# Moving angle and digit work from VectorE to GpSimd, a third pair sum, later low parts and longer values products in a ViT layer kernel

## The reference, cut to what matters

```python
# S4 kernel per token t, for every position l < 1024 and batch c
K = einsum('chn,hnl->chl', Wc, exp(dt_Lambda[..., None] * pos - P_max)).real   # Wc = x * num / den
h = K
h = h + attn(layernorm(h))     # 32 heads of 32, 8 kv groups, rope, causal softmax, T = 128, D = 1024
h = h + ffn(layernorm(h))      # routed low rank: 8 x 16
```

## Time and profile before

| | us |
|---|---|
| median of 3 runs | 2391.71 (2391.33 to 2392.13) |
| the profiled execution, whole | 2390.53 |
| its span | 2388.7 |
| mean granted TensorE clock | 0.988 of full speed |
| busy: TensorE / VectorE / ScalarE / GpSimd | 2276.2 / 1908.7 / 1836.2 / 1708.1 |
| s4_stage, first to last product | 42.2 to about 255.7 |
| layer_stage, first product | 270.0 |
| landing of a 256 KB store of h (DMA list of the page, median) | 3.5 |

### The profile page before, as it was taken

One profiled execution on the slowest core, in us unless ns is written; L12 is line 12 of the kernel. 1 busy time (PEld: TensorE's weight loads), 2 busy tenths in 40 slices (PEclk: granted clock), 3 DMA queues, 4 the chain that ended last, 5 costly groups with the idle time before them and its releaser, 6 DMA issues.

```text
span 2388.7 us, 58825 instructions
## 1 busy us (share of the span) xinstructions
PE 2276.2 (95%) x18704; PEld 1246.2 (52%) x18704; DVE 1908.7 (80%) x7797; ACT 1836.2 (77%) x6269; POOL 1708.1 (72%) x1529
## 2 busy tenths in 40 slices
PE   2999689999999999999999999999999999999986
PEld 2777345555555555555555555555555555555543
DVE  8999578888788788888788878888888878888864
ACT  5998388777877777878777787777787777778773
POOL 1444187877777777777787777777777777777772
PEclk9999899999999999999999999999999999999997
DMA  2888599999999999999999999999999999999984
GB/s 77 263 252 240 135 172 186 187 186 191 189 185 194 188 183 193 191 187 185 191 184 190 192 190 186 189 193 177 192 191 187 187 193 190 180 196 186 184 170 100
DMA packets 1201602, 443.65 MB, mean 186 GB/s; under 512 B 1151622, under 2 KB 1153926, under 8 KB 1201292
## 3 DMA queue, kind: packets, MB, share of 16 engines
q1 hardware_dynamic: 1201284, 439.89, 91.5%
q10 hardware_dynamic: 8, 0.01, 0.0%
HBM read 87.40 MB, written 67.11 MB: 65 GB/s over the span
## 4 chain that ended last, share of the span: by engine, by line
PE 83%; ACT 2%; POOL 1%; DMA 1%; DVE 1%; issue 1%; POOLq 0%; DVEq 0%; ACTq 0%
PE pc L907 13%; PE pb L907 13%; PE pa L907 13%; PE s_ps L920 5%; PE pb L893 4%; PE pb L895 4%; PE pb L894 4%; PE pa L893 4%; PE pa L894 4%; PE pa L895 4%; PE pv_ps L935 4%; PE pd L893 2%; PE pd L895 1%; PE pd L894 1%; DMA pt<-p 1%; ACT pr L1059 1%
## 5 line engine op out<-in xcount | busy, mean ns | idle before, releaser
L1059 ACT ACTIVATE pr<-pr,smin 128x128 f32<-128x128 f32 x2048 | 793.5, 388 | 235.9 <-DVE smin L1205 235.7
L1425 POOL TENSOR_TENSOR pr<-pr,rinv 128x512 f32<-128x512 f32 x512 | 577.0, 1137 | 424.2 <-DVE rinv L1213 413.5
L1205 DVE CUSTOM_DVE_ANT_0 pr<-s_ps,cst 128x128 f32<-128x128 f32 x2048 | 468.7, 286 | 180.2 <-PE s_ps L920 95.7
L1433 POOL TENSOR_TENSOR p<-pr,p 128x512 f16<-128x512 f32 x512 | 590.1, 1158 | 23.9 <-ACT p L1069 13.0
L1069 ACT ACTIVATE p<-pr 128x512 f16<-128x512 f32 x512 | 319.0, 623 | 181.0 <-POOL pr L1425 153.4
L1059 ACT ACTIVATION_READ_ACCUMULATOR pr<-pr,smin 128x1 f32 x2048 | 382.1, 187 | 0.0
L907 PE MATMUL pa<-wkv_hi,xt 128*128 128x512 f16 x1024 | 326.3, 380 | 14.8 <-DMA xt<-xs 14.8
L907 PE MATMUL pb<-wq_hi,xt 128*128 128x512 f16 x1024 | 326.6, 380 | 0.0
L907 PE MATMUL pc<-wq_hi,xt 128*128 128x512 f16 x1024 | 315.0, 379 | 0.0
L642 PE MATMUL hps<-z,xw 128*128 128x256 f32 x848 | 193.7, 388 | 62.1 <-POOL xw L348 42.2
L642 PEld LDWEIGHTS hps<-z,xw 128*128 128x128 f32 x848 | 162.4, 194 | 92.9 <-POOL xw L348 50.5
(11 more groups left out here) (188 smaller groups left out, 4896.2 us busy)
## 6 DMA issues: line engine op xcount, KB each, us to landing
h<-rows SPq DMA_DIRECT2D x128, 256.0 KB, 3.5
h_res<-h SPq DMA_DIRECT2D x64, 512.0 KB, 4.5
out<-rows SPq DMA_DIRECT2D x64, 512.0 KB, 3.2
h_ln<-h SPq DMA_DIRECT2D x63, 512.0 KB, 4.2
pt<-p SPq DMA_TRANSPOSE x512, 3.8
xa<-x SPq DMA_DIRECT2D x16, 256.0 KB, 4.1
xb<-x SPq DMA_DIRECT2D x32, 128.0 KB, 3.8
wst<-wq SPq DMA_DIRECT2D x8, 512.0 KB, 5.7
```

Of the source, the lines that this page charges most:

```text
L1059: last = A.activation(p, p, ACT.Exp, bias=smin[g % 2][:, j:j + 1], scale=-1.0, accum_out=rsum[g % 2][:, j:j + 1])
L1205: V.tensor_tensor_reduce(pr[g % 2][:, cols], s_ps[g % 2][:, cols], mask, 1.0, 3e38, ALU.add, ALU.min, smin[g % 2][:, j:j + 1]).then_inc(ma ...
L1425: nc.gpsimd.tensor_tensor(p3, p3, rinv[g % 2][:, :].unsqueeze(2).broadcast_to([P, HG, P]), ALU.mult).then_inc(p_norm, 1)
L1433: nc.gpsimd.tensor_tensor(p[:, HG * P:], pr[g % 2][:, :], p[:, 0:HG * P], ALU.subtract).then_inc(pl_done, 1)
```

## The change

- Angles are kept in turns instead of radians (zi carries 1/(2 pi)). Bringing them into range is now in_range(): one rounding step (add and subtract MAGIC) and one subtraction; GpSimd does both for chunks 1 to 7, after first_angles. angles() is gone. ScalarE's sines scale by TURN, its square by ROOT_2, so that tables() is one fused step.
- GpSimd makes the second digit product too (digits_m2), right after digits_m1. Its waits on w_lo are gone.
- ON_ACT is 2 in all windows: VectorE makes the xa-products of two tokens a window, ScalarE of two.
- SUM_AT is (0, 1, 2): three of a chunk's eight pairs are summed instead of two.
- pi has two buffers, wst three (WR); low parts are made one window later (LOW_LATER), the last one behind the loop.
- values() in the layer stage waits for its four groups first and then runs 12 matmuls of 512 columns, group g % 4 going to its own 32 partitions of pv_ps; rows of wo are permuted on the host to match.

```diff
-ON_ACT = 3
+WR = 3
+LOW_LATER = 1
+ON_ACT = (2, 2)
...
-        pi = sb("pi", [P, WIN, TOPS, NB])
+        pi = [sb(f"pi{i}", [P, WIN, TOPS, NB]) for i in range(2)]
-        TV, TA, TP = 10, 3, 3
-        SUM_AT = (1, 3)
+        TV, TA, TP = 3, 3, 6
+        SUM_AT = (0, 1, 2)
...
+        def in_range(eng, k):
+            eng.wait_ge(tab_p, TP * k + 1)
+            eng.tensor_scalar(turns[:, :, :], theta[:, :, :], MAGIC, MAGIC, ALU.add, ALU.subtract).then_inc(tab_p, 1)
+            eng.wait_ge(tab_p, TP * k + 2)
+            return eng.tensor_tensor(theta[:, :, :], theta[:, :, :], turns[:, :, :], ALU.subtract)
...
+        def digits_m2(eng, k):
+            return eng.tensor_tensor(dm2[:, :, :].rearrange("p t (s n) -> p t s n", s=2), across(ss, k, 2, DIG),
+                                     tab[k % 2][:, :, :, 0:DIG], ALU.mult)
...
-                    if n >= 2:
-                        sp.wait_ge(w_lo, n - 1)
+                    if n >= WR:
+                        sp.wait_ge(w_lo, n - WR + 1)
...
-                    while loaded < len(PIECES) and PIECES[loaded - 2][0] <= w:
+                    while loaded < len(PIECES) and PIECES[loaded - WR][0] + LOW_LATER <= w + 1:
...
-                        lows = sum(piece[0] < w - 1 for piece in PIECES)
-                        if at in (0, 2, 3) and lows:
-                            pool.wait_ge(w_lo, lows)
                         if at == 0:
-                            pool.wait_ge(tab_v, TV * k + 10)
+                            pool.wait_ge(tab_v, TV * k + 3)
                             first_angles(nc.gpsimd, k + 1).then_inc(tab_p, 1)
+                            in_range(nc.gpsimd, k + 1).then_inc(tab_p, 1)
...
                             digits_m1(nc.gpsimd, k + 1).then_inc(tab_p, 1)
+                            digits_m2(nc.gpsimd, k + 1).then_inc(tab_p, 1)
...
-                    V.tensor_scalar(half[:, :, :], half[:, :, :], -2.0, 1.0, ALU.mult, ALU.add).then_inc(tab_v, 1)
...
-                    V.tensor_tensor(tab[k % 2][:, :, 0, :], expo[:, k * TC:k * TC + TC, :], half[:, :, :],
-                                    ALU.mult).then_inc(tab_v, 1)
+                    V.scalar_tensor_tensor(tab[k % 2][:, :, 0, :], half[:, :, :], 1.0,
+                                           expo[:, k * TC:k * TC + TC, :], ALU.subtract, ALU.mult).then_inc(tab_v, 1)
...
-                    if w >= 1:
-                        dve.wait_ge(xw_done, w)
+                    if w >= 2:
+                        dve.wait_ge(xw_done, w - 1)
...
-                step(V.tensor_scalar(pk, yi, INV_2PI, MAGIC, ALU.mult, ALU.add))
-                step(V.tensor_scalar(pk, pk, MAGIC, None, ALU.subtract))
-                step(V.scalar_tensor_tensor(pf, pk, -TWO_PI_HI, yi, ALU.mult, ALU.add))
-                step(V.scalar_tensor_tensor(pf, pk, -TWO_PI_LO, pf, ALU.mult, ALU.add))
-                step(V.tensor_scalar(pf, pf, PI_SAFE, -PI_SAFE, ALU.min, ALU.max))
+                step(V.tensor_scalar(pk, yi, MAGIC, MAGIC, ALU.add, ALU.subtract))
+                step(V.tensor_tensor(pf, yi, pk, ALU.subtract))
...
-                        if at == 0:
-                            angles(k + 1)
...
-                        if piece[0] == w:
+                        if piece[0] + LOW_LATER == w:
                             weight_lo(n)
+                weight_lo(len(PIECES) - 1)
...
-                        to = slice(P * (g % 4), P * (g % 4) + P)
-                        for n, (v, lo) in enumerate(((v_hi[odd], 0), (v_lo[odd], 0), (v_hi[odd], HG))):
-                            for j in range(HG):
-                                last = pe.matmul(pv_ps[j * HD:(j + 1) * HD, to], v[:, g * HD:(g + 1) * HD],
-                                                 pt[g % RP][:, lo + j, :], start=(n == 0), stop=(n == 2))
+                    for n, (v, lo) in enumerate(((v_hi[odd], 0), (v_lo[odd], 0), (v_hi[odd], HG))):
+                        for g in range(4 * m, 4 * m + 4):
+                            strip = slice(HD * (g % 4), HD * (g % 4) + HD)
+                            last = pe.matmul(pv_ps[strip, :], v[:, g * HD:(g + 1) * HD],
+                                             pt[g % RP][:, lo:lo + HG, :], start=(n == 0), stop=(n == 2))
```

More of the change, by code:

```diff
@@ L150, in s4_stage @@
         cst = W["cst"]
-        re_row, im_row, neg_re_row, row_sign = (cst[:, c:c + 1] for c in (C_RE, C_IM, C_NRE, C_SIGN))
+        re_row, im_row, row_sign = (cst[:, c:c + 1] for c in (C_RE, C_IM, C_SIGN))
         z = [sb(f"z{i}", [P, 4, QROW]) for i in range(ZR)]
@@ L162, in s4_stage @@
         hout = [W[f"rows{i}"] for i in range(HR)]
-        wst = [sb(f"wst{i}", [P, KC * AW]) for i in range(2)]
+        wst = [sb(f"wst{i}", [P, KC * AW]) for i in range(WR)]
         top_r = sb("top_r", [P, TOPS, T])
@@ L212, in s4_stage @@
         x_in = [sem(f"x_in{i}") for i in range(XR)]
-        w_in = [sem(f"w_in{i}") for i in range(2)]
+        w_in = [sem(f"w_in{i}") for i in range(WR)]
         w_hi = sem("w_hi")
@@ L244, in loads_until @@
         def loads_until(n):
-            return 16 * sum(PIECES[i][4] for i in range(n % 2, n + 1, 2))
+            return 16 * sum(PIECES[i][4] for i in range(n % WR, n + 1, WR))
         def weight(name, k):
@@ L289, in load_weight @@
                         piece = src if k is None else src[k * P:k * P + P, :]
-                        sp.dma_start(wst[n % 2][:, at:at + piece.shape[1]], piece).then_inc(w_in[n % 2], 16)
+                        sp.dma_start(wst[n % WR][:, at:at + piece.shape[1]], piece).then_inc(w_in[n % WR], 16)
                         at += piece.shape[1]
@@ L420, in _ @@
                 for w in range(LEAD):
-                    for e in range(ON_ACT):
+                    for e in range(ON_ACT[w % 2]):
                         products(w, e)
@@ L427, in _ @@
                     for e in range(WIN):
-                        if e < ON_ACT and w + LEAD < WINDOWS:
+                        if w + LEAD < WINDOWS and e < ON_ACT[(w + LEAD) % 2]:
                             products(w + LEAD, e)
@@ L449, in step @@
                     dve.wait_ge(pre_v, steps[0])
-                def angles(k):
-                    if k == 0:
-                        first_angles(V, k).then_inc(tab_p, 1)
-                    dve.wait_ge(tab_p, TP * k + 1)
-                    V.tensor_scalar(turns[:, :, :], theta[:, :, :], INV_2PI, MAGIC, ALU.mult, ALU.add).then_inc(tab_v, 1)
-                    dve.wait_ge(tab_v, TV * k + 1)
-                    V.tensor_scalar(turns[:, :, :], turns[:, :, :], MAGIC, None, ALU.subtract).then_inc(tab_v, 1)
-                    dve.wait_ge(tab_v, TV * k + 2)
-                    V.scalar_tensor_tensor(theta[:, :, :], turns[:, :, :], -TWO_PI_HI, theta[:, :, :],
-                                           ALU.mult, ALU.add).then_inc(tab_v, 1)
-                    dve.wait_ge(tab_v, TV * k + 3)
-                    V.scalar_tensor_tensor(theta[:, :, :], turns[:, :, :], -TWO_PI_LO, theta[:, :, :],
-                                           ALU.mult, ALU.add).then_inc(tab_v, 1)
-                    dve.wait_ge(tab_v, TV * k + 4)
-                    V.tensor_scalar(theta[:, :, :], theta[:, :, :], PI_SAFE, -PI_SAFE,
-                                    ALU.min, ALU.max).then_inc(tab_v, 1)
                 def tables(k):
@@ L544, in _ @@
                 step(V.tensor_scalar(zr[:, :], dt_v[:, :, 0], lam_p[:, 0:1], None, ALU.mult),
-                     V.tensor_scalar(zi[:, :], dt_v[:, :, 1], lam_p[:, 1:2], None, ALU.mult))
+                     V.tensor_scalar(zi[:, :], dt_v[:, :, 1], lam_p[:, 1:2], INV_2PI, ALU.mult, ALU.mult))
                 def lengthened(row):
@@ L599, in _ @@
                 step(V.tensor_scalar(t0, gi, im_row, None, ALU.mult),
-                     V.scalar_tensor_tensor(ss[:, :], gi, neg_re_row, t1, ALU.mult, ALU.subtract))
+                     V.scalar_tensor_tensor(ss[:, :], gi, re_row, t1, ALU.mult, ALU.add))
                 step(V.scalar_tensor_tensor(rr[:, :], gr, re_row, t0, ALU.mult, ALU.subtract))
```

71 lines of the change are left out of this document (36 added, 35 removed).

## The result

The changed kernel takes 2367.73 us, the median of 4 runs (2366.32 to 2370.08), against 2391.52 for the kernel before beside it. The ratio is 0.9904, with a 95% interval from 0.9887 to 0.9921. The forecast was 2366, its range 2349 to 2379, so the time is faster by more than the 0.2% that can be told. The profiled execution took 2367.69 us with a span of 2365.9, 22.8 us less than before.

What follows compares the result with a forecast made beforehand. VectorE's pace plus waits for ScalarE bounds the stage before the layers, TensorE the layer stage. Savings of 20.4 and 5 us, 25.5 in sum, off the profiled 2390.5, lying 1.2 below the median, gave 2366 us, range 2349 to 2379.

Steps and rivals of the forecast that it cites:

- Start and first window: Before the steady chunks: fewer angle steps save 3.7 us at the start and 4.0 us in the first window.
- VectorE's chunk without contention: Steady chunk on VectorE: 26.63 us, less 5.74 removed, plus 1.79 added, gives 22.7 us.
- Contention: Steady chunk: GpSimd's instructions hold VectorE's sums, 1.6 us at the first, 2.1 in total, making a chunk of 24.8 us.
- I take 1.05: GpSimd's chunk: assumed time in us of the rounding, which no row showed, put between VectorE's 0.42 and GpSimd's 1.28.
- I am wrong if the sum isn't held (22.7): Stated failure sign: VectorE's first sum in a chunk is not held by GpSimd, and the chunk takes 22.7 us.
- Seven periods: Chunk periods after the first window: 185.6 us falls to 175.1 at 24.8 each with end corrections, saving 10.5 us.
- Last three windows: End of the stage before the layers: a 1.63 wait goes, a low part moves, 0.54 comes; saves 2.2 us.
- The held store: SyncE's second store waits behind a weight load: cost taken 0; as a rival 2376 to 2378 us, chance 0.06.
- The values products: Layer stage: 12 matmuls in three rounds of 0.215 make a block 0.75 instead of 0.79 us, saving 5 us.
- partial overlap: Rival in the layer stage: strips overlap only partly, a round takes 0.27 instead of 0.215; about 2387 us, chance 0.04.
- serial strips: Rival in the layer stage: long matmuls on different strips run one after another; some 2613 us, chance 0.06.
- the 32.18 to 32.1: Layer stage sign: the period of a batch was to fall from 32.18 to 32.1 us.

Runs made afterwards that it cites:

- the last run: Changed kernel plus rounding on VectorE, loads behind both stores, GpSimd's subtraction after its add and wkv_lo, earlier sines, window 0's sum before rounding: 2356.54 us, ratio 0.9866.

## Why the prediction was right

The time lies 1.7 us from the forecast, and the span fell by 22.8 us where the sum said 25.5. One term was 4.2 us too large; 1.1 us that no step had priced, and 0.5 over three others, made up part of it. Of the forecast steps that came out, one did so by chance: the layer stage's 5.1 us are 3.0 of products and 2.1 of a tail that no step had priced.

- **Start and first window, 7.7 forecast, 8.0 measured.** The eleven angle steps became five, as priced, and the sum of window 0 took 0.87.
- **VectorE's chunk without contention, 22.7.** Confirmed by the last run: its 23.05 us hold an extra rounding step of 0.53, which leaves 22.5, with nearly no holds in it. The waits for ScalarE's high parts went as said.
- **Contention, 2.1 a chunk; period 24.8.** Measured 24.89, so 2.2 to 2.4. The size was right, and the place wrong. The failed step is "I take 1.05" for the rounding on GpSimd: it takes 1.92, outside the bounds of 0.42 and 1.28. These 0.9 us let the add come after the sum instead of ahead of it, and it held wkv_lo by 2.15. (This is worked out from the rows; no run has a shorter rounding and nothing else.) By its own sign, "I am wrong if the sum isn't held (22.7)", the prediction had the place wrong, and that the period agreed even so is in part luck: the same instructions in other orders gave 24.5 and 25.9.
- **Seven periods, 10.5 forecast, 6.3 measured.** This is the mis-sized term. Six steady chunks agree (the second and third last 26.09 and 26.03, with the extra low part of 1.17 each; the last 23.31 where 23.9 was put). The first lasts 29.19 instead of 24.8. The prediction gave it the steady period; its window 2 takes 4.1 more, where the sines come late, with wq's high part (1.05) and a table load of 1.28 us ahead of them on ScalarE, and the add behind them holds wq_lo. The last run, with the sines early and the other moves, shows this window at 6.54.
- **Last three windows, 2.2 forecast, 2.3 measured.** Right. The further 1.1 us up to the layer stage's first product was not priced, and no run looked into it.
- **The held store, 0.** Right, and for the reason given. ScalarE waits up to 2.1 us for stores, 21.0 us in all between 60 and 220, and taking 16 us of these away (loads behind the stores) left the period at 24.90.
- **The values products, 5.** The round was right at 0.22, which removes the rivals of partial overlap and of serial strips. The term was too large: 3.0 us in either direction of the test, since a block became 0.022 us shorter and not 0.04. The other 2 us of the layer stage's gain are the tail at the higher clock. The period of a batch went from 32.29 to 32.24; the 32.18 to 32.1 that the prediction named were an average over the stage and not a batch's.

The Trainium skill, SBUF — State Buffer, "SBUF: two separate sides", spoke against the change: an exclusive lock for a whole instruction. These traces agree in each hold shown here, down to its length; they don't for GpSimd's rounding, beside which a sum of VectorE took 0.87 us with 1.6 us of the rounding left. The page gave no size; that came from laying out the two timelines.

The Trainium skill, TensorE: Matmul & The Clock Gate, Part 3, "The mechanism", says that matmuls start in strict program order. The strip-by-strip run disagrees, and the measurement decides: here three products of one strip, issued before those of the next, didn't hold them back.

## What to carry to other kernels

Where instructions of two engines hold each other up, as here GpSimd's adds and VectorE's two-operand steps, the cost is neither the sum of their work nor a property of one step: write both timelines side by side, find what releases each GpSimd instruction, and look where its end falls among the other engine's two-operand steps. A single hold taken away moves the rest; only when the late release behind it (here ScalarE's sines) was moved as well did the chunk come down to VectorE's own 23.05 us. (The two runs that did it moved four things at once; what each is worth among them wasn't measured.) Measure too which steps hold each other: the rounding, nearly as long as an add, hardly held the sum. And price the first turn of a loop by itself: sines that come late there, behind a function table to load, cost 4.1 us here, about the whole error of the seven periods.

## What the runs showed that was not expected

- A rounding step of GpSimd (two scalar operations on one 512-wide operand) takes 1.92 us alone, longer than its products and subtractions of two operands of the same size (1.05 and 1.27), and 4.5 times VectorE's 0.43.
- Products on different 32-column strips start out of the program's order: a block took 0.76 us with the rounds outside and 0.78 with the strips outside, where strict order would have given 2.0.
- VectorE's two-operand sum ran beside GpSimd's rounding with a hold of 0.2 us at most, in seven traces, while a GpSimd add of two operands held such steps for all of its rest.
- The last 37 us of the program took 2 us more or less with the granted clock of that stretch, 0.73 or 0.85 of full speed, for the same instructions.
- A one-operand step of VectorE is still held, as the row at 44.19 of the kernel before had shown: the rounding took 2.57 us beside GpSimd's add in the last run's first chunk, and 0.61 otherwise. The wide products for pi, xw and z were held in no row read here.
